# The MLP in two sweeps of two token chunks each, instead of one sweep of four

## The chip, the cores and the metric

One core of a Trainium2 chip runs the whole kernel. The engines are TensorE (PE, with its weight loads PEld), VectorE (DVE), ScalarE (ACT), GpSimd (POOL) and the DMA queues, here issued from SyncE (SP). The metric is the time of one execution on the device in microseconds; of several runs the median is given.

## The reference, cut to what matters

A batch of 8 x 256 = 2048 tokens of 512 features goes through a first non-local attention block and then through two cross attentions and an MLP, each behind a layer norm and with a residual. The change touches the MLP and the norm ahead of it:

```python
x = res + _cross_attention(h, xf_2, wq2, ..., bias_v2)
h = _layer_norm(x, ln_mlp_scale, ln_mlp_offset)          # 2048 x 512
h = gelu(h @ w_fc1 + b_fc1) @ w_fc2 + b_fc2              # 512 -> 2048 -> 512
return x + h
```

## The kernel before

All float32 products are made of three float32r matmuls: each operand is split in a high part (a cast) and a low part (a subtract), and `product` (lines 781 to 783) adds high*high, high*low and low*high in PSUM. Splits of weights are GpSimd's: `halve` casts (line 580) and subtracts (line 583) a raw block of 128 x 1024 that a DMA brought to `raw`. Splits of activations are ScalarE's (cast) and VectorE's (subtract).

The tokens lie in four chunks of 512. The MLP's 2048 hidden columns lie in eight blocks of 256. A step m is one block for one chunk: f(m) is fc1 (24 matmuls into two PSUM banks, one for each half of 128 columns), then ScalarE's gelu into `tmp` (L1103) and cast into `gT` (L1111), then VectorE's subtract into `gT` (L1368); W(m) is fc2, four tiles of six matmuls, each added to the residual `x` by VectorE (L1377). Before, m runs over the four chunks within a block, and over the eight blocks once: 32 steps. `last_order` puts f(m+1) ahead of W(m).

TensorE, ScalarE and VectorE follow one written list of units (`last_order` is its end). TensorE's results go round a ring of four PSUM banks U: a unit takes the bank of the unit four places before it, and waits until that one is free (`take`). The bank of half i of an f is free when VectorE has made its gT, a bank of W when VectorE has added it.

The layer norm of a chunk: GpSimd or VectorE writes the normalised rows to `z`, TensorE turns them in four groups of four transposes (Z, `rows`, L852), ScalarE applies scale and offset and casts, VectorE subtracts into `hT` (L1358). For the MLP, chunks 0 and 1 are turned in the last two steps of the attention, chunks 2 and 3 in and around W(0) and W(1).

A block's weights sit in `wqs` / `wqs_c` (fc1) and `wos` / `wos_c` (fc2), alternating. GpSimd's queue is `queries(E+1)`, `outputs(E+1)` for each block: the split of the fc1 weights waits for the last f of the block that used the buffer, the split of the fc2 weights for its last W. In between GpSimd adds the output bias to x once for each chunk (`add_bias`, L714), which waits for the chunk's first W. SyncE loads the next raw block as soon as a split has freed `raw`, and stores the output at the end.

Of the kernel before, what the change touches and what calls it, by code (L numbers as in the profile page):

```python
# [40 lines left out]
CH = D // P  # L41
LAYERS = 2
BODIES = H // 2
# [5 lines left out]
CHUNKS = 4  # L49
TILES = B * TOK // P  # L50
GROUPS = HBODIES // 2
STEPS = HBODIES * CHUNKS
MSTEPS = MBODIES * CHUNKS
ITEMS = 4 * STEPS
RING = 4
PAIRS = CHUNKS // 2
# [92 lines left out]
    return out  # L149


def norm_at(s):

    for n in range(NORMS):
        c = s - 2 - (n * BODIES * CHUNKS - CHUNKS)
        if 0 <= c < CHUNKS:
            return n, c
    return None
# [27 lines left out]
def last_order():  # L186

    def f(m, i):
        return [("f", m, i, half) for half in range(2)] if m < MSTEPS else []

    def rows(c):
        return [("Z", LAYERS, c, ch) for ch in range(CH)]

    def mixed(m, c, before):

        out = []
        for t in range(4):
            out += [rows(c)[ch] for ch in before[t]] + [("W", m, t)]
        return out

    out = [("P", ITEMS - 1)] + f(1, 0) + [("w", STEPS - 1, 2), ("w", STEPS - 1, 3)] + f(1, 1)
    out += mixed(0, 2, ((0,), (1,), (2,), (3,))) + f(2, 0) + f(2, 1) + mixed(1, 3, ((), (0, 1), (2,), (3,)))
    for m in range(2, MSTEPS):
        out += f(m + 1, 0) + f(m + 1, 1) + [("W", m, t) for t in range(4)]
    return out


# [33 lines left out]
def bass_xattn(nc, x_in, ctx_in, thw, thb, pgw, pgb, www, bncol, wa, wk, wv, wb, hcol, vrow,  # L241
               lncol, f1col, orow, out):
    ctx = ExitStack()
    with ctx:
# [6 lines left out]
        def f(ap):  # L251

            return ap.bitcast(F32)
# [161 lines left out]
        def _(sp):  # L415
            def load(i, E, src):

                if E:
                    sp.wait_ge(split[i], E)
                else:  # L420
                    sp.wait_ge(k_form, 7 * (quad(ROUNDS - 1, i) + 1))
                sp.dma_start(raw[i][:], src).then_inc(raw_in[i], 16)

            def load_o(E):
                load(1, E, wb[E].rearrange("p c (a n) -> p (c a) n", n=256))

            def load_key_weights(r, i):

# [115 lines left out]
            for E in range(HBODIES):  # L544
                for c in range(CHUNKS):
                    s = E * CHUNKS + c + 1
                    if 1 < s < STEPS:
                        load_k(s)
                        load_values(s)
                    if c == 2:  # L550
                        load(0, E + 2, wa[E + 2])
                    if c == 1:
                        load_o(E + 1)
                        if E in (2, BODIES + 2):
                            bias_row(1 + E // BODIES)
            for E in range(HBODIES, HBODIES + MBODIES - 1):
                load_o(E + 1)
                if E + 2 < HBODIES + MBODIES:
                    load(0, E + 2, wa[E + 2])
            for c in range(CHUNKS):  # L560
                for t in range(4):
                    sp.wait_ge(free, FREE["W", MSTEPS - CHUNKS + c, t] + 1)
                    sp.dma_start(out[c, t], x[:, 4 * c + t, :]).then_inc(stored, 16)
            sp.wait_ge(stored, 16 * TILES)

# [2 lines left out]
        def _(pool):  # L568
# [91 lines left out]
            def queries(E):  # L660

                if E == 0:
                    pool.wait_ge(unit, UNIT["K", ROUNDS - 1, 1, P4] + 1)
                elif E == 1:
                    pool.wait_ge(staged, len(KV))
                elif E <= HBODIES:
                    pool.wait_ge(unit, UNIT["q", (E - 1) * CHUNKS - 1, 1] + 1)
                elif E == HBODIES + 1:
                    pool.wait_ge(logit, ITEMS)
                else:  # L670
                    pool.wait_ge(unit, UNIT["f", (E - 1 - HBODIES) * CHUNKS - 1, 1] + 1)
                w = query_weights(E)
                halve(0, E, w[:, 0], w[:, 1], raw[0][:])

            def outputs(E):

                if E == 0:
                    pool.wait_ge(unit, UNIT["K", ROUNDS - 1, 1, P4] + 1)
                elif E <= HBODIES:
                    pool.wait_ge(unit, UNIT["w", E * CHUNKS - 1, 3] + 1)  # L680
                elif E == HBODIES + 1:
                    pool.wait_ge(pv, ITEMS)
                else:
                    pool.wait_ge(unit, UNIT["W", (E - 1 - HBODIES) * CHUNKS - 1, 3] + 1)
                w = output_weights(E)
                halve(1, E, w[:, 0], w[:, 1], raw[1][:].rearrange("p (c a) n -> p c (a n)", c=2))

# [20 lines left out]
            def add_bias(n, c):  # L708

                pool.wait_ge(brow_in, n * 16 + 16)  # L710
                first = ("w", n * BODIES * CHUNKS + c, 3) if n < LAYERS else ("W", c, 3)
                pool.wait_ge(free, FREE[first] + 1)
                for t in range(4 * c, 4 * c + 4):
                    pool.tensor_tensor(x[:, t, :], x[:, t, :], brow[:], ALU.add).then_inc(ln_bias, 1)  # L714
# [33 lines left out]
            for E in range(HBODIES):  # L748
# [13 lines left out]
                if last:  # L762
                    if n < LAYERS:
                        normalise(n, 3)
                    else:
                        deviation(n, 3)
            for E in range(HBODIES, HBODIES + MBODIES - 1):
                queries(E + 1)
                if E == HBODIES:
                    for c in range(3):  # L770
                        add_bias(LAYERS, c)
                outputs(E + 1)
                if E == HBODIES:
                    add_bias(LAYERS, 3)


        @block.tensor
        def _(pe):
# [75 lines left out]

            def projected(what, s, h, half):

                c = s % CHUNKS
                E = s // CHUNKS + (HBODIES if what == "f" else 0)
                fresh = s % (BODIES * CHUNKS) < CHUNKS
                if half == 0:  # L860
                    if c == 0 and h == 0:
                        pe.wait_ge(split[0], E + 1)
                    take(what, s, h)
                if h == 0 and fresh:
                    pe.wait_ge(free, FREE["Z", E // BODIES, c, 2 * half + 1] + 1)
                o = bank(what, s, h)
                for ch in (2 * half, 2 * half + 1):
                    mm = product(o, parts(query_weights(E), ch, slice(h * P, h * P + P)), parts(hT[c], ch), ch == 0, ch == CH - 1)
                if half == 1:
                    mm.then_inc(unit, 1)  # L870

            def output(what, s, t):
                E = s // CHUNKS + (HBODIES if what == "W" else 0)
                if s % CHUNKS == 0 and t == 0:
                    pe.wait_ge(split[1], E + 1)
                if what == "w" and t in (0, 2):
                    pe.wait_ge(o_done, 4 * s + t + 2)
                if what == "W" and t == 0:
                    pe.wait_ge(free, FREE["f", s, 1] + 1)
                o = take(what, s, t)  # L880
                src = oT if what == "w" else gT[s % 2]
                for h in range(2):
                    mm = product(o, parts(src, h, slice(t * P, t * P + P)), parts(output_weights(E), h, slice(0, D)), h == 0, h == 1)
                mm.then_inc(unit, 1)
# [107 lines left out]
        def _(act):  # L992
# [103 lines left out]
                act.activation(qT[:, 0, h, :], bank("q", s, h), ACT.Identity, bias=hc[:, 0, at_:at_ + 1]).then_inc(hi, 1)  # L1096

            def hidden(m, i):
                at_ = 2 * (m // CHUNKS) + i
                act.wait_ge(unit, UNIT["f", m, i] + 1)  # L1100
                if m:
                    act.wait_ge(free, FREE["f", m - 1, i] + 1)
                act.activation(tmp[:, i, :], bank("f", m, i), ACT.Gelu, bias=f1c[:, at_:at_ + 1]).then_inc(gelu, 1)  # L1103
                if m > 1 and i == 0:
                    act.wait_ge(unit, UNIT["W", m - 2, 3] + 1)
                elif m == 0 and i == 0:
                    act.wait_ge(logit, ITEMS - 4)
                elif m == 1 and i == 0:
                    act.wait_ge(pv, ITEMS - 4)
                act.wait_ge(gelu, GELU["f", m, i] + 1)  # L1110
                act.activation(gT[m % 2][:, 0, i, :], tmp[:, i, :], ACT.Copy).then_inc(g_hi, 1)  # L1111
# [88 lines left out]
        def _(dve):  # L1200
# [167 lines left out]
                dve.tensor_tensor(gT[m % 2][:, 1, i, :], tmp[:, i, :], f(gT[m % 2][:, 0, i, :]), ALU.subtract).then_inc(free, 1)  # L1368

            def output(what, s, t):  # L1370
                tile = 4 * (s % CHUNKS) + t
                if t == 0 and what == "w" and s % (BODIES * CHUNKS) // CHUNKS == 1:
                    dve.wait_ge(ln_bias, s // (BODIES * CHUNKS) * TILES + 4 * (s % CHUNKS) + 4)
                if t == 0 and what == "W" and s // CHUNKS == 1:
                    dve.wait_ge(ln_bias, LAYERS * TILES + 4 * (s % CHUNKS) + 4)
                dve.wait_ge(unit, UNIT[what, s, t] + 1)
                dve.tensor_tensor(x[:, tile, :], x[:, tile, :], bank(what, s, t), ALU.add).then_inc(free, 1)  # L1377

# [165 lines left out]
```

## Time and profile before

| | us |
|---|---|
| median of 3 runs | 2357.95 (2356.15 to 2360.07) |
| profiled execution | 2355.32 |
| its span, first to last instruction | 2353.5 |
| PE busy | 2308.7 (98%) |
| DVE busy | 1488.8 (63%) |
| ACT busy | 1177.4 (50%) |
| POOL busy | 892.9 (38%) |

The span is the time from the first to the last instruction; the execution's own time is 1.8 us more. An engine's busy time says how much work it has; what bounds the time is read from the chain that ended last and from the waits of the engine that is on it. The MLP stands at the end, from about 1990 us on. TensorE's mean granted clock is 0.997 of full speed.

### The profile page before, as it was taken

The numbers are of one execution on the slowest core, as the hardware profiler recorded it, in microseconds if no ns is written. First come the engines' busy times: TensorE is split into PE (matmuls) and PEld (weight loads), VectorE is DVE, ScalarE is ACT, GpSimd is POOL, SyncE is SP. The second block draws the span as 40 slices with busy tenths as digits, with TensorE's granted clock in tenths as the row PEclk, the third lists the DMA queues.
The fourth block names the chain that finished last, engine by engine and source line by source line (L and its number), as shares of the span: only waits on it lengthen the run. The fifth ranks groups of instructions, "written<-read, shape, count | busy, mean of one in ns | idle before, by whom it ended". The sixth has DMA issues, their size and how long they took to land.

```text
span 2353.5 us, 33519 instructions
## 1 busy us (share of the span) xinstructions
PE 2308.7 (98%) x12144; PEld 1961.7 (83%) x12144; DVE 1488.8 (63%) x2444; ACT 1177.4 (50%) x2897; POOL 892.9 (38%) x876
## 2 busy tenths in 40 slices
PE   7999999999999999999999999999999998999999
PEld 4888888788887788888888878888888887788887
DVE  4777767777777666666666776666666666534433
ACT  3322224322323866666666677666666667322222
POOL 5787876688786430011100253211101114611110
PEclk9999999999999999999999999999999999999999
DMA  4677775577777433333334323343334330100001
GB/s 169 233 269 271 266 278 198 197 251 280 268 267 252 159 121 134 131 126 123 138 121 141 126 85 124 133 141 125 117 126 143 128 134 29 34 30 27 28 1 72
DMA packets 147937, 352.88 MB, mean 150 GB/s; under 512 B 9536, under 2 KB 75584, under 8 KB 131392
## 3 DMA queue, kind: packets, MB, share of 16 engines
q1 hardware_dynamic: 147056, 350.65, 42.9%
q8 instruction: 99, 1.62, 0.3%
q14 instruction: 62, 0.51, 0.1%
q10 hardware_dynamic: 720, 0.10, 0.0%
HBM read 211.78 MB, written 138.94 MB: 149 GB/s over the span
## 4 chain that ended last, share of the span: by engine, by line
PE 87%; ACT 5%; DVE 3%; issue 2%; POOL 2%; DMA 0%; SPq 0%; DVEq 0%; ACTq 0%; POOLq 0%
PE U L781 22%; PE U L783 22%; PE U L782 22%; PE T L909 4%; PE O L781 2%; PE O L783 2%; PE S L783 2%; PE O L782 2%; PE S L781 2%; PE S L782 2%; ACT probs L1125 1%; ACT aff L1084 1%; POOL z L705 1%; ACT probs L1117 1%; DVE hT L1358 1%
## 5 line engine op out<-in xcount | busy, mean ns | idle before, releaser
L580 POOL CAST wos<-raw 128x1024 fp32r<-128x1024 f32 x20 | 20.9, 1047 | 852.9 <-PE U L783 852.9
L1377 DVE TENSOR_TENSOR x<-x,U 128x512 f32<-128x512 f32 x384 | 261.2, 683 | 80.8 <-PE U L783 78.6
L1385 DVE TENSOR_REDUCE nm<-S 128x2 f32<-128x514 f32 x256 | 177.3, 693 | 123.4 <-PE S L783 119.6
L1117 ACT ACTIVATE probs<-S,nm 128x257 f32<-128x257 f32 x512 | 237.7, 476 | 27.2 <-DVE nm L1385 27.2
L1135 ACT ACTIVATE PT<-T 128x512 fp32r<-128x512 f32 x256 | 152.5, 596 | 173.3 <-PE T L909 172.8
L1125 ACT ACTIVATE probs<-probs,rs 128x256 f32<-128x256 f32 x512 | 230.1, 500 | 0.5 <-DVE rs L1389 0.5
L1400 DVE SCALAR_TENSOR_TENSOR oT<-O,hc,oT 128x256 fp32r<-128x256 f32 x256 | 123.8, 484 | 143.1 <-ACT oT L1144 143.1
L781 PE MATMUL U<-wos,oT 128*128 128x512 f32 x512 | 213.4, 417 | 0.3 <-DVE gT L1368 0.2
L1072 ACT ACTIVATE stage<-tmp 128x512 fp32r<-128x512 f32 x128 | 81.1, 633 | 243.9 <-DVE tmp L1350 235.5
L783 PE MATMUL U<-wos,oT 128*128 128x512 f32 x512 | 202.0, 395 | 0.0
L1393 DVE TENSOR_TENSOR PT<-T,PT 128x512 fp32r<-128x512 f32 x256 | 175.5, 686 | 41.8 <-ACT PT L1135 41.8
L782 PE MATMUL U<-wos,oT 128*128 128x512 f32 x512 | 201.3, 393 | 0.0
L781 PE MATMUL U<-wvs,plain 128*128 128x512 f32 x512 | 201.0, 393 | 0.0
L783 PE MATMUL U<-wvs,plain 128*128 128x512 f32 x512 | 200.0, 391 | 0.0
L782 PE MATMUL U<-wvs,plain 128*128 128x512 f32 x512 | 199.9, 390 | 0.0
L1144 ACT ACTIVATE oT<-O,hc 128x256 fp32r<-128x256 f32 x256 | 121.2, 473 | 126.3 <-PE O L783 126.3
L1066 ACT ACTIVATE stage<-z 128x512 fp32r<-128x512 f32 x128 | 81.0, 633 | 196.2 <-DVE z L1311 195.7
L1353 DVE TENSOR_TENSOR stage<-tmp,stage 128x512 fp32r<-128x512 f32 x128 | 107.3, 839 | 102.1 <-ACT stage L1072 102.1
L1103 ACT ACTIVATE tmp<-U,f1c 128x512 f32<-128x512 f32 x64 | 44.0, 688 | 246.1 <-PE U L783 246.0
L909 PE MATMUL T<-ident,probs 128*128 128x128 f32 x1024 | 155.2, 274 | 11.4 <-ACT probs L1125 11.0
L1368 DVE TENSOR_TENSOR gT<-tmp,gT 128x512 fp32r<-128x512 f32 x64 | 57.1, 893 | 165.7 <-ACT gT L1111 165.7
L781 PE MATMUL U<-hT,wqs 128*128 128x512 f32 x384 | 155.7, 405 | 2.4 <-DVE hT L1358 2.4
(196 smaller groups left out, 6717.2 us busy)
## 6 DMA issues: line engine op xcount, KB each, us to landing
kd<-stage SPq DMA_DIRECT2D x128, 516.0 KB, 3.7
kb<-kd SPq DMA_DIRECT2D x64, 1032.0 KB, 4.8
vd<-stage SPq DMA_DIRECT2D x128, 512.0 KB, 5.2
vb<-vd SPq DMA_DIRECT2D x64, 1024.0 KB, 5.0
raw<-wk SPq DMA_DIRECT2D x32, 512.0 KB, 4.9
rawv<-wv SPq DMA_DIRECT2D x28, 512.0 KB, 6.2
raw<-wa SPq DMA_DIRECT2D x24, 512.0 KB, 5.9
raw<-wb SPq DMA_DIRECT2D x24, 512.0 KB, 5.9
```

Source lines behind the costliest of these rows:

```text
L781: pe.matmul(o, lhs[0], rhs[0], start=start, stop=False)
L782: pe.matmul(o, lhs[0], rhs[1], start=False, stop=False)
L783: return pe.matmul(o, lhs[1], rhs[0], start=False, stop=stop)
L909: mm = pe.transpose(T[:, at_:at_ + P], probs[:, J % 2, qt, tt * P:tt * P + P], ident[:])
L1117: ins = act.activation(probs[:, r, qt, 0:257], S[:, qt, 0:257], ACT.Exp, bias=nm[:, r, qt:qt + 1], scale=-1.0, accum_out=sums[:, r, qt:qt ...
L1125: ins = act.activation(probs[:, r, qt, 0:256], probs[:, r, qt, 0:256], ACT.Copy, scale=rs[:, r, qt:qt + 1])
L1135: act.activation(PT[:, J % 2, 0, :], T[:], ACT.Copy).then_inc(pt_hi, 1)
L1144: act.activation(oT[:, 0, h, b * 256:b * 256 + 256], O[:, 0:256], ACT.Identity, bias=hc[:, 3, at_:at_ + 1]).then_inc(o_hi, 1)
L1377: dve.tensor_tensor(x[:, tile, :], x[:, tile, :], bank(what, s, t), ALU.add).then_inc(free, 1)
L1385: dve.tensor_reduce(nm[:, J % 2, :], S[:, :, 0:257], AX.X, ALU.min).then_inc(least, 1)
L1393: dve.tensor_tensor(PT[:, J % 2, 1, :], T[:], f(PT[:, J % 2, 0, :]), ALU.subtract).then_inc(pt, 1)
L1400: dve.scalar_tensor_tensor(out=oT[:, 1, h, to], in0=O[:, 0:256], scalar=hc[:, 3, at_:at_ + 1], in1=f(oT[:, 0, h, to]), op0=ALU.add, op1=AL ...
```

## The change

The steps of the MLP are numbered in another way: `hidden_of(m)` gives chunk and block of step m, and the first 16 steps are all eight blocks for chunks 0 and 1, the second 16 all eight blocks for chunks 2 and 3. So each block's weights are loaded and split twice (`stored_at` names the block in DRAM for the sixteen loads), each time used for two steps; the waits of GpSimd's splits count two steps for a block. The Z of chunk 2 go one by one into W(2) to W(5), those of chunk 3 into W(8) to W(11), each behind the second of W's four tiles. The bias is added for two chunks at each sweep's start.

```diff
+SWEPT = CHUNKS // 2 * MBODIES
...
+def hidden_of(m):
+
+    return 2 * (m // SWEPT) + m % 2, m % SWEPT // 2
+
+
+def mlp_step(c, e):
+    return c // 2 * SWEPT + 2 * e + c % 2
...
-    def mixed(m, c, before):
-
-        out = []
-        for t in range(4):
-            out += [rows(c)[ch] for ch in before[t]] + [("W", m, t)]
-        return out
-
+    turned = {2 + ch: ("Z", LAYERS, 2, ch) for ch in range(CH)}
+    turned.update({8 + ch: ("Z", LAYERS, 3, ch) for ch in range(CH)})
     out = [("P", ITEMS - 1)] + f(1, 0) + [("w", STEPS - 1, 2), ("w", STEPS - 1, 3)] + f(1, 1)
-    out += mixed(0, 2, ((0,), (1,), (2,), (3,))) + f(2, 0) + f(2, 1) + mixed(1, 3, ((), (0, 1), (2,), (3,)))
-    for m in range(2, MSTEPS):
-        out += f(m + 1, 0) + f(m + 1, 1) + [("W", m, t) for t in range(4)]
+    for m in range(MSTEPS):
+        if m:
+            out += f(m + 1, 0) + f(m + 1, 1)
+        out += [("W", m, 0), ("W", m, 1)] + ([turned[m]] if m in turned else []) + [("W", m, 2), ("W", m, 3)]
     return out
...
-            for E in range(HBODIES, HBODIES + MBODIES - 1):
+            for E in range(HBODIES, HBODIES + 2 * MBODIES - 1):
                 load_o(E + 1)
-                if E + 2 < HBODIES + MBODIES:
-                    load(0, E + 2, wa[E + 2])
+                if E + 2 < HBODIES + 2 * MBODIES:
+                    load(0, E + 2, wa[stored_at(E + 2)])
...
-                    pool.wait_ge(unit, UNIT["f", (E - 1 - HBODIES) * CHUNKS - 1, 1] + 1)
+                    pool.wait_ge(unit, UNIT["f", (E - 1 - HBODIES) * 2 - 1, 1] + 1)
...
-                    pool.wait_ge(unit, UNIT["W", (E - 1 - HBODIES) * CHUNKS - 1, 3] + 1)
+                    pool.wait_ge(unit, UNIT["W", (E - 1 - HBODIES) * 2 - 1, 3] + 1)
...
-            for E in range(HBODIES, HBODIES + MBODIES - 1):
+            for E in range(HBODIES, HBODIES + 2 * MBODIES - 1):
                 queries(E + 1)
-                if E == HBODIES:
-                    for c in range(3):
-                        add_bias(LAYERS, c)
                 outputs(E + 1)
-                if E == HBODIES:
-                    add_bias(LAYERS, 3)
+                if (E - HBODIES) % MBODIES == 0:
+                    for c in range(2):
+                        add_bias(LAYERS, 2 * ((E - HBODIES) // MBODIES) + c)
```

TensorE before, at the start of W(0): `U<-hT,wqs` is the end of f(1), `U<-ident,z` a Z, `U<-wos,gT` W(0), six matmuls for a tile.

```order
L783 MATMUL U<-hT_54,wqs 128x512
L852 MATMUL U<-ident,z 128x128 x4
L781 MATMUL U<-wos,gT_82 128x512
L782 MATMUL U<-wos,gT_82 128x512
L783 MATMUL U<-wos,gT_82 128x512
L781 MATMUL U<-wos,gT_82 128x512
L782 MATMUL U<-wos,gT_82 128x512
L783 MATMUL U<-wos,gT_82 128x512
L852 MATMUL U<-ident,z 128x128 x4
```

TensorE after, in W(2), the first place in which a Z stands now (lines have moved by six: 787 to 789 are `product`, 858 is `rows`); it is between the second and the third tile.

```order
L787 MATMUL U<-wos_c,gT_82 128x512
L788 MATMUL U<-wos_c,gT_82 128x512
L789 MATMUL U<-wos_c,gT_82 128x512
L858 MATMUL U<-ident,z 128x128 x4
L787 MATMUL U<-wos_c,gT_82 128x512
L788 MATMUL U<-wos_c,gT_82 128x512
L789 MATMUL U<-wos_c,gT_82 128x512
```

A Z ahead of each tile of W(0) has become one Z in the middle of a W, with an f and four tiles between two of them.

GpSimd before, from the split of the MLP's second block on: casts and subtracts are splits, `x<-x,brow` the bias adds, four for a chunk.

```order
L580 CAST wqs_c<-raw 128x1024
L583 TENSOR_TENSOR wqs_c<-raw,wqs_c 128x1024
L714 TENSOR_TENSOR x<-x,brow 128x512 x12
L580 CAST wos_c<-raw 128x1024
L583 TENSOR_TENSOR wos_c<-raw,wos_c 128x1024
L714 TENSOR_TENSOR x<-x,brow 128x512 x4
L580 CAST wqs<-raw 128x1024
L583 TENSOR_TENSOR wqs<-raw,wqs 128x1024
L580 CAST wos<-raw 128x1024
L583 TENSOR_TENSOR wos<-raw,wos 128x1024
```

GpSimd after, from the same place.

```order
L588 CAST wqs_c<-raw 128x1024
L591 TENSOR_TENSOR wqs_c<-raw,wqs_c 128x1024
L588 CAST wos_c<-raw 128x1024
L591 TENSOR_TENSOR wos_c<-raw,wos_c 128x1024
L722 TENSOR_TENSOR x<-x,brow 128x512 x8
L588 CAST wqs<-raw 128x1024
L591 TENSOR_TENSOR wqs<-raw,wqs 128x1024
L588 CAST wos<-raw 128x1024
L591 TENSOR_TENSOR wos<-raw,wos 128x1024
```

The second block's fc2 split stands ahead of the bias adds, and only two chunks' bias adds stand ahead of the third block's splits; the other two chunks' stand at the same place of the second sweep. Splits follow one another twice as closely.

## Rows read from the trace of the kernel before

**Rows 1.** The page: an engine's busy time; the chain that ended last.
```profile
PE 2308.7 (98%) x12144; PEld 1961.7 (83%) x12144; DVE 1488.8 (63%) x2444; ACT 1177.4 (50%) x2897; POOL 892.9 (38%) x876
...
PE 87%; ACT 5%; DVE 3%; issue 2%; POOL 2%; DMA 0%; SPq 0%; DVEq 0%; ACTq 0%; POOLq 0%
```
**Rows 2.** Waits from 1985 us: who waited for whom, total, times, longest.
```profile
ACT tmp L1103 <- PE U L783: 246.0, 62, 7.2
...
PEld U L781 <- DVE gT L1368: 3.4, 7, 0.5
```
**Rows 3.** Timeline at W(0): start, us, engine, line, out<-in [idle before <-releaser].
```profile
2002.85 0.60 PE L852 MATMUL U<-ident,z 128*128 128x128 f32 x4
...
2003.93 0.50 PE L781 MATMUL U<-wos,gT 128*128 128x512 f32 x1 [0.48 <-POOL wos L583]
```
**Rows 4.** Timeline, TensorE in W(1); the last row is W(2)'s first.
```profile
2018.38 1.04 PE L852 MATMUL U<-ident,z 128*128 128x128 f32 x8
...
2019.71 0.51 PE L781 MATMUL U<-wos,gT 128*128 128x512 f32 x1 [0.30 <-DVE gT L1368]
...
2021.22 0.60 PE L852 MATMUL U<-ident,z 128*128 128x128 f32 x4
...
2021.57 0.48 PE L781 MATMUL U<-wos,gT 128*128 128x512 f32 x1
...
2023.06 0.60 PE L852 MATMUL U<-ident,z 128*128 128x128 f32 x4
...
2030.36 0.39 PE L781 MATMUL U<-wos,gT 128*128 128x512 f32 x1
```
**Rows 5.** Timeline, the first matmuls of W(22), W(26) and W(30).
```profile
2251.17 0.40 PE L781 MATMUL U<-wos_c,gT 128*128 128x512 f32 x1
...
2295.36 0.39 PE L781 MATMUL U<-wos,gT 128*128 128x512 f32 x1
...
2339.24 0.40 PE L781 MATMUL U<-wos_c,gT 128*128 128x512 f32 x1
```
**Rows 6.** Timeline of W(6), all engines: a split and VectorE's subtract.
```profile
2074.24 0.40 PE L781 MATMUL U<-wos_c,gT 128*128 128x512 f32 x1
...
2074.47 1.04 POOL L580 CAST wqs_c<-raw 128x1024 fp32r<-128x1024 f32 x1 [13.85 <-PE U L783]
...
2075.59 2.40 POOL L583 TENSOR_TENSOR wqs_c<-raw,wqs_c 128x1024 fp32r<-128x1024 f32 x1
...
2075.82 2.72 DVE L1368 TENSOR_TENSOR gT<-tmp,gT 128x512 fp32r<-128x512 f32 x1 [1.97 <-ACT gT L1111]
...
2078.15 0.40 PE L783 MATMUL U<-wos_c,gT 128*128 128x512 f32 x1
...
2078.59 0.19 PEld L781 LDWEIGHTS U<-wos_c,gT 128*128 128x128 f32 x1 [0.48 <-DVE gT L1368]
2078.60 0.50 PE L781 MATMUL U<-wos_c,gT 128*128 128x512 f32 x1
```
**Rows 7.** Timeline, GpSimd's first split, then its last bias adds in W(4).
```profile
2006.10 2.73 POOL L583 TENSOR_TENSOR wqs_c<-raw,wqs_c 128x1024 fp32r<-128x1024 f32 x1
...
2047.87 5.48 POOL L714 TENSOR_TENSOR x<-x,brow 128x512 f32<-128x512 f32 x4 [1.75 <-DVE x L1377]
...
2053.89 0.99 DVE L1368 TENSOR_TENSOR gT<-tmp,gT 128x512 fp32r<-128x512 f32 x1 [1.69 <-ACT gT L1111]
...
2054.41 2.74 POOL L583 TENSOR_TENSOR wqs<-raw,wqs 128x1024 fp32r<-128x1024 f32 x1
...
2057.82 0.40 PE L781 MATMUL U<-hT,wqs_c 128*128 128x512 f32 x1
```
**Rows 8.** Line 1368 from 2060 us: ns min/median/max; who waited for it, times.
```profile
L1368 DVE TENSOR_TENSOR gT<-tmp,gT x52: 691/693/2718, 2062.2 to 2340.8; 128x512 fp32r<-128x512 f32 x52
...
  PEld U L781: 2.5, 5
```
**Rows 9.** DMA from 2000 us: KB each, median us to landing.
```profile
raw<-wb SPq DMA_DIRECT2D x7, 512.0 KB, 3.4
```

More of the change, by code:

```diff
@@ L189, in f @@
         return [("f", m, i, half) for half in range(2)] if m < MSTEPS else []
-    def rows(c):
-        return [("Z", LAYERS, c, ch) for ch in range(CH)]
-    def mixed(m, c, before):
-        out = []
-        for t in range(4):
-            out += [rows(c)[ch] for ch in before[t]] + [("W", m, t)]
-        return out
+    turned = {2 + ch: ("Z", LAYERS, 2, ch) for ch in range(CH)}
+    turned.update({8 + ch: ("Z", LAYERS, 3, ch) for ch in range(CH)})
     out = [("P", ITEMS - 1)] + f(1, 0) + [("w", STEPS - 1, 2), ("w", STEPS - 1, 3)] + f(1, 1)
-    out += mixed(0, 2, ((0,), (1,), (2,), (3,))) + f(2, 0) + f(2, 1) + mixed(1, 3, ((), (0, 1), (2,), (3,)))
-    for m in range(2, MSTEPS):
-        out += f(m + 1, 0) + f(m + 1, 1) + [("W", m, t) for t in range(4)]
+    for m in range(MSTEPS):
+        if m:
+            out += f(m + 1, 0) + f(m + 1, 1)
+        out += [("W", m, 0), ("W", m, 1)] + ([turned[m]] if m in turned else []) + [("W", m, 2), ("W", m, 3)]
     return out
@@ L422, in load, with stored_at @@
                 sp.dma_start(raw[i][:], src).then_inc(raw_in[i], 16)
+            def stored_at(E):
+                return E if E < HBODIES else HBODIES + (E - HBODIES) % MBODIES
             def load_o(E):
-                load(1, E, wb[E].rearrange("p c (a n) -> p (c a) n", n=256))
+                load(1, E, wb[stored_at(E)].rearrange("p c (a n) -> p (c a) n", n=256))
             def load_key_weights(r, i):
@@ L555, in _ @@
                             bias_row(1 + E // BODIES)
-            for E in range(HBODIES, HBODIES + MBODIES - 1):
+            for E in range(HBODIES, HBODIES + 2 * MBODIES - 1):
                 load_o(E + 1)
-                if E + 2 < HBODIES + MBODIES:
-                    load(0, E + 2, wa[E + 2])
+                if E + 2 < HBODIES + 2 * MBODIES:
+                    load(0, E + 2, wa[stored_at(E + 2)])
             for c in range(CHUNKS):
                 for t in range(4):
-                    sp.wait_ge(free, FREE["W", MSTEPS - CHUNKS + c, t] + 1)
+                    sp.wait_ge(free, FREE["W", mlp_step(c, MBODIES - 1), t] + 1)
                     sp.dma_start(out[c, t], x[:, 4 * c + t, :]).then_inc(stored, 16)
@@ L710, in add_bias @@
                 pool.wait_ge(brow_in, n * 16 + 16)
-                first = ("w", n * BODIES * CHUNKS + c, 3) if n < LAYERS else ("W", c, 3)
+                first = ("w", n * BODIES * CHUNKS + c, 3) if n < LAYERS else ("W", mlp_step(c, 0), 3)
                 pool.wait_ge(free, FREE[first] + 1)
@@ L855, in projected @@
             def projected(what, s, h, half):
-                c = s % CHUNKS
-                E = s // CHUNKS + (HBODIES if what == "f" else 0)
-                fresh = s % (BODIES * CHUNKS) < CHUNKS
+                if what == "q":
+                    c, E, n, fresh = s % CHUNKS, s // CHUNKS, s // CHUNKS // BODIES, s % (BODIES * CHUNKS) < CHUNKS
+                else:
+                    c, E, n, fresh = hidden_of(s)[0], HBODIES + s // 2, LAYERS, s % SWEPT < 2
                 if half == 0:
-                    if c == 0 and h == 0:
+                    if h == 0 and s % (CHUNKS if what == "q" else 2) == 0:
                         pe.wait_ge(split[0], E + 1)
@@ L864, in projected @@
                 if h == 0 and fresh:
-                    pe.wait_ge(free, FREE["Z", E // BODIES, c, 2 * half + 1] + 1)
+                    pe.wait_ge(free, FREE["Z", n, c, 2 * half + 1] + 1)
                 o = bank(what, s, h)
@@ L872, in output @@
             def output(what, s, t):
-                E = s // CHUNKS + (HBODIES if what == "W" else 0)
-                if s % CHUNKS == 0 and t == 0:
+                E = s // CHUNKS if what == "w" else HBODIES + s // 2
+                if s % (CHUNKS if what == "w" else 2) == 0 and t == 0:
                     pe.wait_ge(split[1], E + 1)
@@ L1098, in hidden @@
             def hidden(m, i):
-                at_ = 2 * (m // CHUNKS) + i
+                at_ = 2 * hidden_of(m)[1] + i
                 act.wait_ge(unit, UNIT["f", m, i] + 1)
@@ L1370, in output @@
             def output(what, s, t):
-                tile = 4 * (s % CHUNKS) + t
+                tile = 4 * (s % CHUNKS if what == "w" else hidden_of(s)[0]) + t
                 if t == 0 and what == "w" and s % (BODIES * CHUNKS) // CHUNKS == 1:
                     dve.wait_ge(ln_bias, s // (BODIES * CHUNKS) * TILES + 4 * (s % CHUNKS) + 4)
-                if t == 0 and what == "W" and s // CHUNKS == 1:
-                    dve.wait_ge(ln_bias, LAYERS * TILES + 4 * (s % CHUNKS) + 4)
+                if t == 0 and what == "W" and hidden_of(s)[1] == 1:
+                    dve.wait_ge(ln_bias, LAYERS * TILES + 4 * hidden_of(s)[0] + 4)
                 dve.wait_ge(unit, UNIT[what, s, t] + 1)
```

## The prediction

> **What bounds the kernel now.** I read the page's busy shares and its chain first. TensorE is busy 98% of the span and holds 87% of the chain [rows 1], so a change moves the time only where it makes TensorE wait or lets it stop waiting. Then the table of waits for the stretch from 1985 us on, where the MLP stands: long idle times of the other engines, but for TensorE only fractions of a microsecond, mostly "PEld U <- DVE gT", 7 times, at most 0.5 us each [rows 2]. The MLP is a chain of matmuls with small holes. So the prediction is a list of holes: those that go, those that come, and those that are copied.
>
> I call a step one pair f, W: f(m) is 24 matmuls (fc1, 256 hidden columns, one chunk of 512 tokens), W(m) is 24 more (fc2) in four tiles of six. A step without a hole takes 10.97 us: the first matmuls of W(26) and W(30), four steps apart and behind the last weight split, stand at 2295.36 and 2339.24, 43.88 us apart [rows 5]. An f or a W is half, 5.48 us, a tile of W 1.37 us.
>
> **Part 1: the norm's transposes leave the join.** Before, eight groups of four transposes (Z, line 852) stand from before W(0) to W(1). TensorE reaches W(0) and waits for GpSimd's split of the fc2 weights until 2003.93 [rows 3]. From there to the first matmul of W(2) at 2030.36 [rows 4] it takes 26.43 us, in which W(0), f(2), W(1), f(3) and seven Z stand. The two steps are 21.94 us. The price of one Z inside a W: from one Z to the next 2021.22 to 2023.06 is 1.84 us [rows 4], a tile of W is 1.37, so 0.47 us. Seven are 3.29. What is left, 26.43 - 21.94 - 3.29 = 1.20 us, are holes; the largest is behind the double Z, where 8 transposes at 2018.38 are followed by a matmul at 2019.71 that waited for VectorE's gT [rows 4]. In the changed order none of the Z stands there, VectorE and ScalarE have only their usual work, and these holes go: -1.20 us. The eighth Z (2002.85) filled time in which TensorE waited for the split anyway; its release at 2003.93 doesn't move, since GpSimd's queue up to there is the same. Moved behind, this Z now costs: +0.47 us. Sum of part 1: -0.73 us. Next late there is the split of block 1's fc1 weights, which the new order needs at f(2), 2003.93 + 5.48 = 2009.41, instead of at f(4). GpSimd ends it at 2006.10 + 2.73 = 2008.83 [rows 7], so nothing waits, with 0.6 us to spare. That block's fc2 weights are wanted at W(2); GpSimd now splits them ahead of the bias adds, and their load, issued as the first fc2 split ends, takes 3.4 us [rows 9]. Nothing waits.
>
> **Part 2: the splits are doubled.** A block of weights is now used for two steps, not four, and there are 16, not 8: 8 more loads for each matrix (512 KB in 3.4 us [rows 9], one of each kind in 22 us, on DMA queues that are nearly empty here) and 16 more pairs of a cast (1.04 us) and a subtract (2.40 us) on GpSimd [rows 6], 6.9 us of work in 22 us. That load by itself fits. Its price is what a split does to VectorE. In rows 6 GpSimd is released by the end of f(7) and starts its subtract at 2075.59; VectorE's subtract for gT is issued at 2075.82 and takes 2.72 us, where 0.69 is the median [rows 8], and ends only after GpSimd. W waits for it: in the ring of four PSUM banks the fourth tile of W takes the bank of the second half of f. TensorE starts that tile at 2078.60; the matmul before started 0.45 us earlier (0.23 is usual) and the first of the tile takes 0.50 for 0.39. So a hole of 0.22 + 0.11 = 0.33 us. A whole body says the same: from W(22), 2251.17, to W(26), 2295.36, are 44.19 us with one such split [rows 5], 0.31 more than 43.88. Rows 8 count five of them behind 2060 us. The split of the fc2 weights is released by the end of a W and meets no such subtract; it costs nothing, as now.
>
> The Trainium skill ("SBUF — State Buffer", Who interferes with whom) says that a VectorE instruction with two SBUF inputs and a GpSimd instruction that reads SBUF exclude each other for the whole instruction, the earlier one winning. The rows agree: gT<-tmp,gT is held until GpSimd's end, and x<-x,U, with one input in SBUF, isn't. By that rule it is 0.23 us of lead that decides every hole.
>
> Now which splits meet it. The fc1 split of block j (0 to 15) is released by the end of f(2j-3), so it falls into W(2j-4). Before it was f(4j-5), in W(4j-6), j = 3 to 7: five holes. After:
> - j = 5, 8, 9, 12, 13, 14, 15 fall into W(6), W(12), W(14), W(20), W(22), W(24), W(26), which are as before: 7 x 0.33 = 2.31 us.
> - j = 4, 6, 7 fall into W(4), W(8), W(10), and there a Z now stands between the second and the third tile. It takes one bank of the ring, so the bank of f's second half is wanted by the third tile. That one is due 2 x 1.37 + 0.47 = 3.21 us behind W's start; the bank is free as in rows 6, 2078.60 - 2074.24 = 4.36 us behind it. Each is a hole of 1.15 us: 3.45 us. The trace of before shows no Z in such a place; from below the price is 0.33 us (the same hole as without Z), from above 1.15, since VectorE can't be held longer than GpSimd's one subtract. I take 1.15: both ends of the difference are measured times.
> - j = 2 and j = 10 are queued on GpSimd behind the bias adds of two chunks, whose second waits for W(1) or W(17). Before, the same row of things stands at 2047.87 [rows 7]: bias 5.48 us, cast, then VectorE is first (issued 2053.89, 0.99 us) and GpSimd's subtract waits (2.74 us). VectorE is done at 2054.88; W starts 5.48 us before the f at 2057.82, at 2052.34, so the bank is free 2.54 us behind it, early enough even with a Z (3.21). No hole. The split ends at 2057.15 and the f two steps on, which wants the new weights, starts at 2057.82: 0.67 us to spare in W(18), 1.1 in W(2) with its Z. Bounds 0 and 1.15 for j = 2, 0 and 0.33 for j = 10.
> - j = 3 and j = 11 follow right behind those (their loads are there, 3.4 us), in f(4) and f(20). They can hold the subtract of f's first half, whose bank isn't wanted before the following W. Bounds as for j = 2 and 10; I take 0.
> Sum of part 2: 2.31 + 3.45 - 5 x 0.33 = +4.11 us.
>
> **Part 3: the rest.** The stores of chunks 0 and 1 leave after the first sweep's results instead of at the end, but chunk 3 is last as before and its last tile's store closes the span: 0. VectorE's normalisation of chunk 3 (four instructions) now stands in W(5) behind a Z; it holds up only adds of tiles whose banks are wanted a half step later: 0. A bias add of one tile takes 5.48 / 4 = 1.37 us [rows 7] and can hold a gT subtract that long. Unheld, the bank is free 2075.82 + 0.69 - 2074.24 = 2.27 us behind W's start [rows 6], 1.84 before the fourth tile wants it, and no bias add stands at the second gT subtract of a step with a Z: 0.
>
> **Sum.** -0.73 + 4.11 = +3.4 us. The profiled execution took 2355.32 us (span 2353.5) and would take 2358.7; the median of the three runs is 2357.95, 2.6 above it, and goes to 2361.3, or +0.14%. About 0.2% (4.7 us) is what a measurement of this kernel can tell from no change, so this is a loss that mostly reads as none.
>
> **The rivals.**
> - Slower for certain: the four delayed splits (j = 2, 3, 10, 11) meet the subtract too. For it speaks that in rows 7 VectorE is first by only half a microsecond, and that GpSimd's queue at that place has other work in front of it than before. Price 2 x 1.15 in the first sweep (Z steps) and 2 x 0.33 in the second, +2.96: in all +6.3 us, 2364.3. It decides at the start of GpSimd's subtract: before VectorE's request, the hole is there. Against: bias adds and steps have the same lengths as at 2047.87.
> - The Z steps are no worse than the others, if the ring's shift is made good by something that I don't see: 3 x 0.82 less, +0.9 us, 2358.9. Against: the banks are handed out in the order of the program.
> - VectorE gets in first in the new order and GpSimd waits, which harms nobody: all such holes go, -0.73 - 1.65 = -2.4 us, 2355.6. This is what the rule above would give if the 0.23 us of lead were lost. Against: both are released by the same end of f, as in five of five bodies before.
>
> **How the numbers follow.** Forecast 0.60, the slow rival 0.22, level Z steps 0.12, VectorE first 0.06. Forecast: 2361.3, its own spread 2 us (two medians of runs that lie 4 us apart, and the places set at 0). It exceeds +4.7 us in about one case in seven; with the slow rival slower has 0.29. Faster by over 0.2% needs 2353.2, under every sum here; 0.05 for what I haven't seen. Within 0.2%: 0.66. The range goes from 2358.0, which leaves out only the third rival, to 2364.8, which takes in the slow one.
>
> **What would show it.** GpSimd: 30 splits behind W(0)'s start instead of 14. TensorE: a wait "PEld U <- DVE gT" of 0.5 us in W(6), 12, 14, 20, 22, 24, 26 and of about 1.3 us in W(4), W(8), W(10), on the first matmul of the third tile; gT subtracts of 2.7 us in just these steps. W(0) still starts at about 2003.9, W(2) 21.9 us later. No wait for wqs at f(2), f(4), f(20). It is wrong if f waits for a split, if the long gT subtracts stand without a hole in the Z steps, or if TensorE's matmuls themselves become slower.

## The result and the profile after

| | before | changed |
|---|---|---|
| median of 22 runs each, us | 2356.59 | 2361.29 |
| ratio, 95% interval | | 1.0019 (1.0013 to 1.0026) |
| profiled execution / its span, us | 2355.32 / 2353.5 | 2363.05 / 2361.3 |
| W(0)'s first matmul, us | 2003.93 | 2007.69 |
| from there to the end, us | 349.57 | 353.61 |

The changed kernel is slower by 0.19%, about 4.5 us, inside the forecast range. That the forecast time of 2361.3 us was met to 0.01 us is luck: it started from 2357.95 us for the kernel before, 1.36 above the median of 22 runs, and its +3.4 us was 1.3 below the 4.7 us between the two medians. From W(0) on, where the order of work differs (the one Z just ahead of W(0) filled a wait there), the two profiled executions differ by 4.04 us. The 3.8 us by which the changed one reaches W(0) later are not of the change: e1, e2, e3 and e5 below keep its code up to W(0) and reach W(0) at 2004.60, 2006.25, 2004.35 and 2002.71 us. What goes with this spread in the record is TensorE's mean granted clock, 0.997 in the profiled execution before and 0.995 in the changed one, while from 2000 us on both show 1.00. The 22 runs of the changed kernel tend the same way: 2357.55 us at 0.999, 2359.72 to 2361.30 at 0.997, 2364.11 at 0.994. So I compare the stretch from W(0) on, in one profile against another, and take the ratio of the times as the check.

The busy shares, which answer to [rows 1]: TensorE 4.9 us more, VectorE 12.7 and GpSimd 54.7, which are 16 more pairs of a cast and a subtract at 3.44 us.

```profile
PE 2313.6 (98%) x12144; PEld 1966.1 (83%) x12144; DVE 1501.5 (64%) x2444; ACT 1177.6 (50%) x2897; POOL 947.6 (40%) x908
```

The waits from 1985 us of the changed kernel, which answer to [rows 2] (who waited for whom: total, times, longest):

```profile
PEld U L787 <- DVE gT L1375: 7.3, 10, 1.2
PE U L787 <- DVE gT L1375: 3.2, 4, 1.0
...
POOL wqs_c L588 <- DMA raw<-wa: 2.0, 1, 2.0
...
PEld U L787 <- POOL wos L591: 1.3, 1, 1.3
```

Ten waits for gT, not seven, and the longest is 1.2 us, not 0.5. One split waited for its DMA (during f(20)), and nobody waited for that split. The join, TensorE's first matmul of W(0) and of W(2), answers to [rows 3, 4]:

```profile
2007.69 0.50 PE L787 MATMUL U<-wos,gT 128*128 128x512 f32 x1 [0.93 <-POOL wos L591]
...
2029.77 0.40 PE L787 MATMUL U<-wos_c,gT 128*128 128x512 f32 x1
```

From W(0) to W(2) it now takes 22.08 us instead of 26.43 (21.94 forecast), and the wait for the split has grown from 0.48 to 0.93 us, since the Z that filled it is gone.

W(4) is the first of the three steps in which a Z and a fully held gT subtract meet. The timeline (start, duration, engine, line, out<-in, in brackets the idle time before it and its releaser) answers to [rows 6]:

```profile
2052.66 0.39 PE L787 MATMUL U<-wos,gT 128*128 128x512 f32 x1
...
2052.89 1.04 POOL L588 CAST wqs<-raw 128x1024 fp32r<-128x1024 f32 x1 [1.94 <-PE U L789]
...
2054.01 2.38 POOL L591 TENSOR_TENSOR wqs<-raw,wqs 128x1024 fp32r<-128x1024 f32 x1
...
2054.24 2.69 DVE L1375 TENSOR_TENSOR gT<-tmp,gT 128x512 fp32r<-128x512 f32 x1 [1.97 <-ACT gT L1118]
...
2055.38 0.60 PE L858 MATMUL U<-ident,z 128*128 128x128 f32 x4
...
2056.98 0.19 PEld L787 LDWEIGHTS U<-wos,gT 128*128 128x128 f32 x1 [1.24 <-DVE gT L1375]
2056.99 0.50 PE L787 MATMUL U<-wos,gT 128*128 128x512 f32 x1 [1.00 <-DVE gT L1375]
```

GpSimd's subtract starts 0.23 us ahead of VectorE's request, VectorE ends at 2056.93, and the third tile of W starts 1.61 us behind the Z, where 0.35 is usual. That is a hole of 1.26 us; in W(8) and W(10) it is 1.24 and 1.22.

W(2) of the changed kernel shows the other outcome. There the split is late behind the bias adds, as in [rows 7]:

```profile
2030.77 1.03 POOL L588 CAST wqs<-raw 128x1024 fp32r<-128x1024 f32 x1
2031.35 0.99 DVE L1375 TENSOR_TENSOR gT<-tmp,gT 128x512 fp32r<-128x512 f32 x1 [1.69 <-ACT gT L1118]
2031.88 2.73 POOL L591 TENSOR_TENSOR wqs<-raw,wqs 128x1024 fp32r<-128x1024 f32 x1
```

VectorE is first, GpSimd's subtract takes 2.73 us instead of 2.40, and W(2) has no hole.

### The profile page after: what moved, and what is told of

Same layout as the page of the kernel before. It is cut to its first block, busy times and chain, and to the rows that moved or that the text cites. A ratio compares the mean times of both kernels' runs of the same rounds, so it can differ in the third digit from the quotient of the medians.

```text
span 2361.3 us, 33590 instructions
## 1 busy us (share of the span) xinstructions
PE 2313.6 (98%) x12144; PEld 1966.1 (83%) x12144; DVE 1501.5 (64%) x2444; ACT 1177.6 (50%) x2897; POOL 947.6 (40%) x908
## 4 chain that ended last, share of the span: by engine, by line
PE 88%; ACT 5%; DVE 4%; issue 1%; POOL 1%; DMA 0%; SPq 0%; DVEq 0%; ACTq 0%; POOLq 0%
PE U L787 23%; PE U L789 22%; PE U L788 22%; PE T L916 5%; PE O L787 2%; PE S L789 2%; PE O L789 2%; PE S L787 2%; PE O L788 2%; PE S L788 2%; DVE gT L1375 1%; ACT aff L1091 1%; ACT probs L1132 1%; ACT probs L1124 1%; PE S L958 1%
## 5 line engine op out<-in xcount | busy, mean ns | idle before, releaser
L1375 DVE TENSOR_TENSOR gT<-tmp,gT 128x512 fp32r<-128x512 f32 x64 | 70.1, 1095 | 161.9 <-ACT gT L1118 161.9
```

## The experiments

Theory: two subtracts that both read two operands from SBUF, one on GpSimd and one on VectorE, exclude each other. When VectorE comes second, TensorE waits for the bank that it frees; how long is set by which tile takes that bank. The rival causes were the Z themselves, the doubled traffic and work as such, and something ahead of the MLP. The times from W(0) on, each from one profile:

| kernel | W(0) at, us | from W(0) on, us | expected | ratio to before (95%) |
|---|---|---|---|---|
| before | 2003.93 | 349.57 | | |
| changed | 2007.69 | 353.61 | 353.0 | 1.0019 (1.0013 to 1.0026) |
| e1 Z behind third tile | 2004.60 | 351.50 | 350.9 | 1.0010 (1.0001 to 1.0019) |
| e2 Z in odd steps | 2006.25 | 351.05 | 350.9 | 1.0008 (0.9999 to 1.0017) |
| e3 late release | 2004.35 | 347.25 | 347.4 | 0.9988 (0.9979 to 0.9997) |
| e4 doubling alone | 2005.14 | 353.36 | 351.6 | 1.0016 (1.0007 to 1.0025) |
| e5 VectorE first | 2002.71 | 347.29 | 347.4 | 0.9992 (0.9982 to 1.0001) |
| e6 before, late release | 2005.51 | 347.89 | 347.9 | 0.9991 (0.9982 to 0.9999) |
| e7 e3 and a Z at W(0) | 2004.69 | 346.81 | 346.8 | 0.9986 (0.9977 to 0.9995) |

**e1, e2: is it the Z, or where it stands?**

```diff
-        out += [("W", m, 0), ("W", m, 1)] + ([turned[m]] if m in turned else []) + [("W", m, 2), ("W", m, 3)]
+        out += [("W", m, 0), ("W", m, 1), ("W", m, 2)] + ([turned[m]] if m in turned else []) + [("W", m, 3)]
```

> The changed kernel, only that each Z of the first sweep stands behind the third tile of its W, not behind the second. Theory (a hole is GpSimd's subtract holding VectorE's gT, and its size is set by which tile takes the bank of f's second half in the ring of four): the Z itself now takes that bank, at the place in time at which a plain W's fourth tile takes it, so the holes in W(4), W(8), W(10) shrink from about 1.24 us to 0.33: 2.7 us less. From W(0)'s first matmul to the end 353.6 - 2.7 = 350.9 us; against the kernel before +2.0 us (ratio 1.0008). Rival (a transpose group in the middle of a W costs TensorE what it costs wherever it stands): 353.6 and ratio 1.0019.

```diff
-    turned = {2 + ch: ("Z", LAYERS, 2, ch) for ch in range(CH)}
-    turned.update({8 + ch: ("Z", LAYERS, 3, ch) for ch in range(CH)})
+    turned = {1 + 2 * ch: ("Z", LAYERS, 2, ch) for ch in range(CH)}
+    turned.update({9 + 2 * ch: ("Z", LAYERS, 3, ch) for ch in range(CH)})
```

> The changed kernel with the Z in the odd steps, W(1), W(3), W(5), W(7) and W(9), W(11), W(13), W(15), where no split of fc1 weights meets a gT subtract by the count 2j-4. Theory: the holes in W(4), W(8), W(10) become plain ones of 0.33 us, 350.9 us from W(0) on. W(3) has a held subtract of f's first half only and shows no hole. Rival (the Z cost what they cost by themselves): 353.6 us.

Both take away what the theory says, e2 within 0.15 us, e1 within 0.6: 2.6 and 2.1 us less from W(0) on. Against e3 below, which has no holes, e1's W(4), W(8) and W(10) still take 0.52, 0.54 and 0.44 us more, not 0.33 each, and its W(6) 0.65 us (what happens there stands below, at part 3 of the prediction). In e1's W(4) the subtracts collide as in the changed kernel, but now the transposes themselves take the awaited bank, at the time of a plain fourth tile:

```profile
2050.87 2.39 POOL L591 TENSOR_TENSOR wqs<-raw,wqs 128x1024 fp32r<-128x1024 f32 x1
...
2051.11 2.70 DVE L1375 TENSOR_TENSOR gT<-tmp,gT 128x512 fp32r<-128x512 f32 x1 [1.97 <-ACT gT L1118]
...
2053.86 0.42 PEld L858 LDWEIGHTS U<-ident,z 128*128 128x128 f32 x4 [0.52 <-DVE gT L1375]
```

The wait is 0.52 us instead of 1.24, with the same 2.70 us on VectorE. So the same collision costs by its place in the ring; the Z as such is innocent. By their ratios alone e1 and e2 are not told from the changed kernel, the profiles decide here.

**e3, e5: is it the collision, or the doubled work?** e3 releases the fc1 split later, e5 makes VectorE win.

```diff
-                    pool.wait_ge(unit, UNIT["f", (E - 1 - HBODIES) * 2 - 1, 1] + 1)
+                    pool.wait_ge(unit, UNIT["W", (E - 1 - HBODIES) * 2 - 2, 3] + 1)
```

> The changed kernel, only that the split of the fc1 weights of blocks 2 to 15 is released by the end of W(2j-4) instead of the end of f(2j-3), 5.5 us later, where VectorE only adds from PSUM. Theory: no gT subtract is held any more, 3 x 1.24 + 7 x 0.36 = 6.2 us go: 347.4 us from W(0) on, ratio to the kernel before 0.9993 (-1.5 us). The fc1 weights come 5.5 us later and still 22 us early. Rival (the second loading and splitting costs by its traffic or by GpSimd's work as such, wherever it stands): 353.6 us, ratio 1.0019. Rival (the loss lies ahead of the MLP, where the changed kernel's profiled run is 3.8 us late): the MLP's stretch changes, the ratio stays at or above 1.0010.

```diff
-                    pool.wait_ge(unit, UNIT["f", (E - 1 - HBODIES) * 2 - 1, 1] + 1)
+                    pool.wait_ge(free, FREE["f", (E - 1 - HBODIES) * 2 - 1, 1] + 1)
```

> The changed kernel, only that the split of the fc1 weights of blocks 2 to 15 waits until VectorE has made the gT of f(2j-3)'s second half, about 2.3 us later than now, so that VectorE always comes first. Theory (the loser of the two subtracts waits for the whole of the other, and only VectorE's waiting costs): holes gone as with the later release, 353.6 - 6.2 = 347.4 us from W(0) on. The norm's hT subtract of a Z step can be held now, which nobody waits for. Rival (whatever GpSimd does within a W with a Z costs, by hT instead of gT): holes of about 1 us stay in W(4), W(8), W(10), 350.5 us.

Both keep every load, split and matmul of the changed kernel and take 6.3 to 6.4 us from it. Everything that TensorE waited for from 1985 us on in e3:

```profile
PEld T L916 <- ACT probs L1132: 3.0, 1, 3.0
PE T L916 <- ACT probs L1132: 2.8, 1, 2.8
PEld U L787 <- POOL wos L591: 1.3, 1, 1.3
PE U L787 <- POOL wos L591: 0.9, 1, 0.9
PEld U L858 <- issue: 0.2, 1, 0.2
```

No row names gT any more; the rest lies in the attention's last step and at W(0). Three gT subtracts are still held (1.42 us beside a bias add, 2.28 and 1.95 beside the third split of each sweep), but none whose bank TensorE waits for. In e5 a Z step looks like this:

```profile
2049.27 0.69 DVE L1375 TENSOR_TENSOR gT<-tmp,gT 128x512 fp32r<-128x512 f32 x1 [1.97 <-ACT gT L1118]
...
2050.03 1.04 POOL L588 CAST wqs<-raw 128x1024 fp32r<-128x1024 f32 x1 [4.05 <-DVE gT L1375]
...
2051.14 2.41 POOL L591 TENSOR_TENSOR wqs<-raw,wqs 128x1024 fp32r<-128x1024 f32 x1
2052.52 1.58 DVE L1365 TENSOR_TENSOR hT<-aff,hT 128x512 fp32r<-128x512 f32 x1 [1.23 <-ACT hT L1094]
```

VectorE's hT subtract is held now (1.58 us for 0.69), and nothing follows from it, since the bank of a Z is wanted only a half step later. This refutes both rivals: the second loading and splitting is free where it meets no awaited subtract, and since e3's ratio follows the MLP's stretch, nothing is lost ahead of the MLP.

**e4: doubling alone, in the old order.** The functions of the sweep are set back to the old numbering, the Z order is that of the kernel before, a block is still loaded for every two steps:

```diff
-    return 2 * (m // SWEPT) + m % 2, m % SWEPT // 2
+    return m % CHUNKS, m // CHUNKS
...
-    return c // 2 * SWEPT + 2 * e + c % 2
+    return CHUNKS * e + c
...
-                return E if E < HBODIES else HBODIES + (E - HBODIES) % MBODIES
+                return E if E < HBODIES else HBODIES + (E - HBODIES) // 2
...
-                if (E - HBODIES) % MBODIES == 0:
+                if E - HBODIES < 2:
                     for c in range(2):
-                        add_bias(LAYERS, 2 * ((E - HBODIES) // MBODIES) + c)
+                        add_bias(LAYERS, 2 * (E - HBODIES) + c)
```

> One part alone: every block of MLP weights is loaded and split twice (for two chunks each time), but the order is that of the kernel before: one sweep of four chunks, the Z of chunks 2 and 3 in W(0) and W(1). Theory: the join's holes stay, eleven plain steps (W(6), W(8) to W(26)) have a hole of 0.33 us instead of five: 349.6 + 2.0 = 351.6 us from W(0) on, ratio 1.0008. If doubling cost nothing by itself: 349.6 us and 1.0000. If doubling were the whole of the loss: 353.6 us and 1.0019.

A miss: 1.8 us more than expected. The steps behind W(4) came as counted, eleven with a hole against five: 2.20 us more from W(4) to the end than before. What I had left out is the join. There GpSimd now splits the second fc2 block while VectorE works on the Z of chunks 2 and 3, and VectorE's hT is held, for which f(2) waits. The second line shows what is not held: x<-x,U, with one input in PSUM, runs its 0.68 us in the middle of GpSimd's subtract.

```profile
2011.55 2.73 POOL L598 TENSOR_TENSOR wos_c<-raw,wos_c 128x1024 fp32r<-128x1024 f32 x1
2011.94 0.68 DVE L1391 TENSOR_TENSOR x<-x,U 128x512 f32<-128x512 f32 x1
...
2012.80 2.02 DVE L1372 TENSOR_TENSOR hT<-aff,hT 128x512 fp32r<-128x512 f32 x1 [0.19 <-ACT hT L1101]
...
2014.88 0.19 PEld L794 LDWEIGHTS U<-hT,wqs_c 128*128 128x128 f32 x1 [1.04 <-DVE hT L1372]
```

From W(0) to W(2) e4 takes 27.75 us, 1.32 more than before, and f(4) waits for its weights, which stand behind the bias adds: 0.4 us.

```profile
2038.63 0.19 PEld L794 LDWEIGHTS U<-hT,wqs 128*128 128x128 f32 x1 [0.50 <-POOL wqs L598]
```

That e4's loss of 3.79 us comes close to the changed kernel's 4.04 is a coincidence: of e4's only the 2.20 us of plain steps are in the real change too. There the stretches divide in another way: the join gives 0.64 us back (e3 against e6), the doubled splits, all in steps without a Z, cost 2.1 us (e2, 351.05, less e3, 347.25, less the 1.68 us that the holes before cost, by e6 below), and the Z in the steps of the collisions cost another 2.56 (353.61 less e2's 351.05).

**e6, e7: what is left without collisions.**

```diff
-                    pool.wait_ge(unit, UNIT["f", (E - 1 - HBODIES) * CHUNKS - 1, 1] + 1)
+                    pool.wait_ge(unit, UNIT["W", (E - 1 - HBODIES) * CHUNKS - 2, 3] + 1)
```

> The kernel before (one sweep), only that the split of the fc1 weights of blocks 2 to 7 is released by the end of the last W but one of the block whose buffer it takes, 5.5 us later than the end of its last f. Theory: its five holes of 0.33 us go, 349.6 - 1.65 = 347.9 us from W(0) on, ratio 0.9993. Rival (the gain of the late release in the two-sweep order comes from elsewhere): 349.6 us, ratio 1.0000.

e7 is e3 with this:

```diff
+    out += [turned.pop(2)]
     for m in range(MSTEPS):
```

> The two-sweep kernel with the late release (split released by the end of W(2j-4)), and the first Z of chunk 2 back ahead of W(0), where TensorE waits for GpSimd's fc2 split anyway. Theory: this Z is free again, W(0)'s first matmul doesn't move, 347.25 - 0.47 = 346.8 us from W(0) on, ratio to the kernel before 0.9986. Rival (VectorE's and ScalarE's work for this Z delays gT and makes a hole in W(0) or W(1), as before the change): 347.3 us or more.

e6 gives the kernel before its own 1.68 us back. With the collisions out of both orders, e3 against e6 is the first part of the change alone: 347.25 against 347.89, a gain of 0.64 us. e7 fills TensorE's wait for the split with a Z again:

```profile
2003.61 0.60 PE L859 MATMUL U<-ident,z 128*128 128x128 f32 x4
...
2004.69 0.50 PE L788 MATMUL U<-wos,gT 128*128 128x512 f32 x1 [0.49 <-POOL wos L592]
```

The wait is 0.49 us as in [rows 3], the stretch is 0.44 us shorter than e3's. e7, with a median of 2353.84 us against 2356.83 for the kernel before run beside it, beats both kernels. That e7 is better than e3 and e6 is shown by the profiles only; the ratios' intervals overlap.

## Why the prediction was right

- **Part 1, the join (-0.73 us).** Right: -0.64 us between e3 and e6. The holes went, the Z moved behind cost 0.44 us at W(0) (e7 against e3) for a forecast 0.47, and no f waited for a split.
- **Part 2, plain steps (7 x 0.33 = 2.31 us).** Right in place: W(6), 12, 14, 20, 22, 24, 26 and no others. Step by step against e3 they take 2.59 us more. The 0.33 was read at the smaller of two sizes: W(14), 22 and 26, which take 11.00 us without a hole, lose 0.32 each, and W(12), 20 and 24, which take 10.88, lose 0.40 (the 10.97 of the prediction is the mean of four steps of 10.88 to 11.07). W(6) loses 0.44 us, for a reason that part 3 had set at nothing, below.
- **Part 2, Z steps (3 x 1.15 = 3.45 us).** Right in mechanism (e1, e2), a little small in size, and above what was called the upper bound: 3.71 us against e3. The term at fault is the due time of the third tile: I had put it 2 x 1.37 + 0.47 behind W's start, but 0.12 of that 0.47 is the slower tile behind the Z. The tile is due at 3.09 us, and it started 4.33 us behind W's start: 1.24 us each.
- **j = 2, 3, 10, 11 at nothing.** Right in price. In W(2) and W(18) VectorE was first; the splits of j = 3 and 11 held a subtract in f(4) (2.26 us) and in W(19) (1.96 us), without a hole. The second isn't the one foreseen, since its load was not there: it took 5.3 us to land, not 3.4, and GpSimd waited 1.96 us for it. So the split slid out of f(20) and met the subtract of the second half, whose bank was free 3.54 us behind W(19)'s start, 0.6 before the fourth tile took it.
- **Part 3, VectorE's normalisation of chunk 3 at nothing.** Wrong, by 0.1 us. These four instructions have one tensor input, but GpSimd's fc2 split held them: 4.71 us, where the same four take 1.91 in the kernel before, at 2012.21, with GpSimd idle. Not only adds came late by it, as the prediction had it, but the first half's gT subtract too (2076.63). It stood beside GpSimd's cast, which took 1.18 us for 1.04, so GpSimd's subtract ended 3.89 us behind W(6)'s start, not 3.75, and the bank came free that much later. e2 tells that it is the normalisation: there it stands in W(7), and TensorE waits 0.73 us in W(8), where the changed kernel's W(12), a step of the same length, has 0.52, and only 0.48 in W(6).

```profile
2070.81 4.71 DVE L1246 TENSOR_SCALAR z<-x,mv,rstd 128x512 f32<-128x512 f32 x4
2071.56 1.15 POOL L588 CAST wos<-raw 128x1024 fp32r<-128x1024 f32 x1 [15.18 <-PE U L789]
2072.78 2.45 POOL L591 TENSOR_TENSOR wos<-raw,wos 128x1024 fp32r<-128x1024 f32 x1
...
2076.63 0.68 DVE L1375 TENSOR_TENSOR gT<-tmp,gT 128x512 fp32r<-128x512 f32 x1
...
2077.03 1.18 POOL L588 CAST wqs_c<-raw 128x1024 fp32r<-128x1024 f32 x1 [1.80 <-PE U L789]
...
2078.29 2.40 POOL L591 TENSOR_TENSOR wqs_c<-raw,wqs_c 128x1024 fp32r<-128x1024 f32 x1
2078.38 2.86 DVE L1375 TENSOR_TENSOR gT<-tmp,gT 128x512 fp32r<-128x512 f32 x1 [1.07 <-ACT gT L1118]
...
2081.29 0.19 PEld L787 LDWEIGHTS U<-wos_c,gT 128*128 128x128 f32 x1 [0.62 <-DVE gT L1375]
```

- **The sum.** +3.4 us forecast, +4.04 in the profiles from W(0) on, of it 4.68 for the collisions ((353.61 - 347.25) - (349.57 - 347.89)) for a forecast 4.11, less 0.64. The times of 22 runs each say 4.5 us, between 3.1 and 6.1; so the change is told from none, though it was forecast as a loss that mostly reads as none. The chances have a slip too: with a spread of 2 us around +3.4, more than +4.7 comes in about one case in four, not one in seven.
- **The reading of the waits.** The prediction gave TensorE's waits from 1985 us on as at most 0.5 us. The same view has two larger ones ahead of W(0), PEld T <- ACT probs of 3.1 us and PEld O <- issue of 1.0; they stand in the attention's last step, which the change leaves alone.
- **The rivals.** The slow one asked for VectorE to lose at all four delayed splits; it wins at W(2) and W(18), and where it loses, at j = 3 and 11, there is no hole. The level Z steps are refuted by the 1.2 us waits. "VectorE first" didn't happen in the changed kernel, but e5 shows that its price was right: made to happen, it gives 347.29 us, 2.3 less than before for a forecast of 2.4.

## What to carry to other kernels

When an engine is busy 98% of the span, look for a hole that comes back with each pass of a loop, and ask of a change first how many more of these it makes. A helper engine's work that is small and far from late can still stop the bounding engine, by holding one short instruction of a third; moving its release by half a step cost nothing here and took the hole out. And where a ring of buffers hands out banks in program order, a unit put in the middle advances everybody's due time behind it: put it where the awaited bank is already free.

## What the runs showed of the hardware

- A VectorE subtract with two SBUF inputs of 0.69 us takes 2.7 to 2.9 us when a GpSimd subtract of 2.40 us has started before it, even by only 0.09 us (2078.29 and 2078.38 above). In W(2) VectorE's came first, beside GpSimd's cast, and took 0.99; then GpSimd's subtract took 2.73.
- VectorE's float32 tensor_scalar from SBUF to SBUF, with one tensor input, is held by GpSimd too. The Trainium skill ("SBUF — State Buffer", Who interferes with whom) has both: two SBUF inputs, and the 2-port modes that tensor_scalar can enter. The trace agrees in that 4 of these took 4.71 us beside GpSimd's split, and 1.91 us with GpSimd idle; in which mode they ran no run shows.
- Kernels with the same code up to there reach the same matmul at times up to 5 us apart (W(0) at 2002.71 us in e5, with a mean granted clock of 0.998, and at 2007.69 in the changed kernel, with 0.995), while the stretch behind it repeats: e3 and e5, alike in work, differ by 0.04 us there. For a change of 0.1% in a late stage the stage's own stretch tells more than the whole time.
